# Third feed-forward: rounding the gelu rows on ScalarE, and copying the broadcast gates on VectorE

## The reference, cut to what matters

```python
x = x + _L2_ffn_ref(_layernorm(x, axis=-1), L2_ffn_wg, L2_ffn_w1, L2_ffn_b1, L2_ffn_w2, L2_ffn_b2)

def _L2_ffn_ref(x, wg, w1, b1, w2, b2):     # 8 experts, 128 -> 512 -> 128, top 2
    logits = xt.astype(jnp.float32) @ wg.astype(jnp.float32)
    scores = jax.nn.softmax(logits, axis=-1)
    gvals, gidx = jax.lax.top_k(scores, K)
    ...
    gvals = gvals * keep                    # an expert takes at most cap tokens
```

## Time and profile before

| what | value |
|---|---|
| runs | 4552.9, 4552.88 and 4551.13 us, median 4552.88 us |
| profiled execution | span 4550.5 us; no time outside the span is recorded for it |
| busy over the whole span | PE 90%, DVE 86%, ACT 60%, POOL 32% |
| third feed-forward, main loop | 2002.1 to 2811.0 us of the span, 808.9 us, 16 groups |

### The profile page before, as it was taken

How to read it: one execution, slowest core, us unless ns; L and a number is a source line. 1 busy time by engine, 2 the same in 40 slices (tenths; PEclk the granted TensorE clock), 3 DMA queues, 4 the chain that set the end, 5 groups by cost and what they waited for, 6 DMA issues and landing times. The chain is left out here.

```text
span 4550.5 us, 105158 instructions
## 1 busy us (share of the span) xinstructions
PE 4085.3 (90%) x34134; PEld 2858.5 (63%) x34135; DVE 3902.8 (86%) x7025; ACT 2713.1 (60%) x4836; POOL 1476.4 (32%) x779
## 2 busy tenths in 40 slices
PE   6984789994997999869999997999949999699999
PEld 3562556664774666657777775666636666577777
DVE  7888789997996888779999998888868888688888
ACT  3433577772775777535555554777757777366665
POOL 2210055540004555312111213555525555122222
PEclk9976999995998999869999998999969999699999
DMA  1010022221002222200000000222222221100000
GB/s 59 17 46 1 11 68 63 65 49 49 1 0 57 57 59 58 78 24 1 1 0 1 0 1 23 64 55 60 52 64 47 55 50 47 72 15 14 14 14 14
DMA packets 129636, 162.04 MB, mean 36 GB/s; under 512 B 32972, under 2 KB 88593, under 8 KB 128306
## 3 DMA queue, kind: packets, MB, share of 16 engines
q1 hardware_dynamic: 129457, 159.97, 13.3%
HBM read 36.38 MB, written 8.39 MB: 10 GB/s over the span
## 5 line engine op out<-in xcount | busy, mean ns | idle before, releaser
L709 ACT ACTIVATE a_p<-a_p 128x480 f32<-128x480 f32 x832 | 500.7, 602 | 408.0 <-DVE a_p L551 403.8
L1648 DVE TENSOR_TENSOR f_al<-f_a,f_ah 128x512 fp32r<-128x512 f32 x768 | 690.9, 900 | 17.5
L347 POOL TENSOR_TENSOR a_km<-a_k,a_slots 96x1920 fp32r<-96x1920 f32 x186 | 631.8, 3416 | 180.8 <-DMA a_k<-a_kh 180.8
L546 DVE TENSOR_REDUCE a_mx<-a_sc 128x4 f32<-128x480 f32 (+1 forms) x832 | 543.0, 653 | 140.0 <-PE a_sc L802 108.2
L1728 ACT ACTIVATE f_a<-f_pu,f_b 128x512 f32<-128x512 f32 x512 | 353.4, 690 | 374.1 <-PE f_pu L1231 198.6
L551 DVE TENSOR_TENSOR a_p<-a_sc,a_mx 128x480 f32<-128x480 f32 x832 | 531.8, 639 | 18.8
L715 ACT ACTIVATE a_pt<-a_tp 120x512 f32<-120x512 f32 x832 | 486.4, 585 | 76.3 <-PE a_tp L811 73.8
L811 PE MATMUL a_tp<-ident,a_p 128*120 128x128 f32 x3328 | 511.8, 276 | 12.0 <-ACT a_p L709 9.7
L1611 POOL TENSOR_TENSOR f_ya<-f_ya,f_yg 128x512 f32<-128x512 f32 x192 | 254.0, 1323 | 769.1 <-DVE f_yg L1663 466.6
L811 PEld LDWEIGHTS a_tp<-ident,a_p 128*120 128x120 f32 x3328 | 400.3, 138 | 98.8 <-ACT a_p L709 34.8
L796 PE MATMUL a_sc<-a_km,a_qr 96*128 96x480 f32 x768 | 396.2, 516 | 33.0 <-ACT a_qr L704 31.4
(11 more groups left out here) (403 smaller groups left out, 9394.3 us busy)
## 6 DMA issues: line engine op xcount, KB each, us to landing
a_q<-a_qh SPq DMA_DIRECT2D x384, 64.0 KB, 2.0
a_k<-a_kh SPq DMA_DIRECT2D x384, 60.0 KB, 2.0
a_ctx<-in_ctxT SPq DMA_DIRECT2D x64, 240.0 KB, 2.7
a_q<-a_ql SPq DMA_DIRECT2D x192, 64.0 KB, 2.0
a_k<-a_kl SPq DMA_DIRECT2D x192, 60.0 KB, 2.0
s_k<-s_kh SPq DMA_DIRECT2D x128, 64.0 KB, 2.0
s_q<-s_qh SPq DMA_DIRECT2D x128, 64.0 KB, 2.0
x<-in_x SPq DMA_DIRECT2D x4, 1024.0 KB, 7.9
```

The lines of the kernel that those rows point to most:

```text
L347: v.tensor_tensor(KM[par][:, i, :, :].rearrange("p b (j k) -> p b j k", k=KN), K3[:, i, :, :].unsqueeze(2).to_broadcast([TR, GB, 4, KN]), ...
L546: v.tensor_reduce(mx[:], view, AX.X, ALU.max).then_inc(mx_ready, 1)
L709: a.activation(PR[s % 4][:], PR[s % 4][:], ACT.Exp).then_inc(exp_ready, 1)
L1648: v.tensor_tensor(AL[s % 4][:], A[s % 2][:], AH[s % 4][:].bitcast(F32), ALU.subtract).then_inc(Z["lo_ready"], 1)
```

## The change

In the third feed-forward only, `high` moves from VectorE to ScalarE. There it is called one slot later: after the gelu of slot s ScalarE rounds the rows of unit s - 1, as in the fourth feed-forward. `low` on VectorE follows one slot later too. The copy of the broadcast gates out of PSUM, `spread`, moves from ScalarE to VectorE and stands directly ahead of `weigh` in its program. LAG becomes 3. The tiles and their numbers stay: two `A`, four `AH`, four `AL`, two `PU`. In the diff the first hunk is the shared setting, the next three are VectorE's program, the last is ScalarE's.

```diff
-    LAG = 3 if two else 2
+    LAG = 3
...
-                def high(g, s):
-                    n = g * N + s
-                    dve.wait_ge(Z["a_ready"], n + 1)
-                    at_least(dve, Z["dn_ready"], n - 3)
-                    v.tensor_copy(AH[s % 4][:], A[s % 2][:]).then_inc(Z["hi_ready"], 1)
...
+                def spread(g, u):
+                    if u % HB != 0:
+                        return
+                    e = u // HB
+                    dve.wait_ge(Z["ge_ready"], g * E + e + 1)
+                    at_least(dve, Z["yg_ready"], g * E + e - 1)
+                    v.tensor_copy(GX[e % 2][:], PG[:]).then_inc(Z["gx_ready"], 1)
...
                         if two:
                             product(g, s)
-                            lagged(g, s, first, 1, low)
-                        else:
-                            high(g, s)
-                            low(g, s)
+                        lagged(g, s, first, 1, low)
+                        if not two:
+                            lagged(g, s, first, LAG, spread)
                         lagged(g, s, first, LAG, weigh)
...
                 def group(g, par, first, last):
                     for s in range(N):
                         rows(g, s)
+                        lagged(g, s, first, 1, high)
                         if two:
-                            lagged(g, s, first, 1, high)
-                        lagged(g, s, first, LAG, spread)
+                            lagged(g, s, first, LAG, spread)
```

More of the change, by code:

```diff
@@ L1687, in group @@
                     if last:
-                        if two:
-                            low(g, N - 1)
+                        low(g, N - 1)
                         for u in range(N - LAG, N):
+                            if not two:
+                                spread(g, u)
                             weigh(g, u)
@@ L1759, in group @@
                     if last:
+                        high(g, N - 1)
                         if two:
-                            high(g, N - 1)
-                        for u in range(N - LAG, N):
-                            spread(g, u)
+                            for u in range(N - LAG, N):
+                                spread(g, u)
                 gates_in(0, 0)
```

## The result

The changed kernel takes 4878.2 us (median of 4 runs, 4877.3 to 4880.3) against 4552.6 us before: a ratio of 1.0717, 95% interval 1.0704 to 1.0730. It is 326 us slower. The forecast was 4891 us.

A forecast was written before the change was run, and what follows sets the result against it. VectorE was taken to bound the old kernel, a ring of waits the changed one: 1039 + 74 + 15 + 12 and 7 drain make the loop 1147 us, +338 on 4553, so 4891 us; range 4780 to 4950.

The forecast's parts named there:

- The step that decided: Third feed-forward loop: a circle of waits, not engine rates, sets the pace, 2.03 us a unit against 1.58 before.
- the ring: Third feed-forward: gelu n-1, rounding of n-2, low n-2, then gelu n, with two A tiles; 2.03 us a unit.
- the first rival: Circle of waits doesn't bind; TensorE's rate limits the loop to 775 us, kernel 4519 us; 4 in 100.
- turns of the ring: Loop's 512 units, each gelu, rounding, low and handovers one after another at 2.03 us: 1039 us.
- held by GpSimd, slots other than the split's: VectorE's low stretched 0.66 us when it starts 0.51 us into GpSimd's add; 74 us for all 112.
- slot of the split: Slot 10: weigh, cast and the split's subtraction, which meets an add, end about 0.6 us later than counted.
- slot of the residual: Slot 5: VectorE's residual takes 1.76 us, less 0.08, which is 0.34 us too long for the free time.
- turns of the hardware loop: VectorE's 2.49 us stand behind that slot's copy makes low 1.8 us late, seven times: 12 us.
- drain behind the last gelu: End of the third feed-forward loop: work left after the last gelu, 7 us.
- the line read from the earlier trace: Excess of a held low is about 1.17 us minus its offset into GpSimd's add, from two pairs.
- TensorE's clock: Loop: clock stays 1.00 with TensorE about 80% busy; rival: falls to 1.2 GHz, 5159 us, 6 in 100.
- what LAG does: In the loop, LAG at 3 costs only a slot at the end, under 2 us.

The follow-up runs named there:

- the other order: Changed kernel, two A tiles kept, but ScalarE rounds each unit's rows at once, directly behind that unit's own gelu instead of one slot later: 4517.1 us, ratio 0.9921.

## Why the prediction was right

**The step that decided** held: the loop runs at the ring's turn, not at the highest rate. Four A tiles and the other order each open the ring, by different means, and both give TensorE's bound of the first rival: 4523 and 4517 us, for which it had 4519.

**The terms**, in the changed kernel. The measured ones are read from the gaps between all gelus of the loop: 2.025 us is the undisturbed gap, and what a slot's gaps have above it is added up over the 16 groups.

| term | forecast, us | measured, us |
|---|---|---|
| turns of the ring | 512 x 2.03 = 1039 | 510 x 2.025 = 1032.8, and 0.6 between the first two gelus |
| held by GpSimd, slots other than the split's | 96 x 0.66 = 63 | 58.8, about 0.61 each |
| slot of the split | 16 x 1.26 = 20 | 19.6 |
| slot of the residual | 16 x 0.34 = 5 | 4.5 |
| turns of the hardware loop | 12 | 7.4, with all else that the rows above leave |
| drain behind the last gelu | 7 | 3134.7 - 3125.2 = 9.5 |
| loop | 1147 | 1133.2 |

All terms but the drain came out a little below the forecast, so the 13 us between 4891 and 4878 are a sum of small errors and not of large ones that cancel.

One turn stands in the rows as 0.59 (2502.36 to 2502.95), 0.65 for the rounding and its handover (to 2503.60), 0.69 for `low`, and 0.10 to the gelu at 2504.39: 2.03 us. The hold is as reckoned in 49 of the 96 `low` that met an add: they start 0.50 to 0.52 us into it and take 1.32 to 1.34 us, 0.63 to 0.65 too much, where the forecast had 0.51 and 0.66. One of them:

```profile
2252.36 1.29 POOL L1611 TENSOR_TENSOR f_ya<-f_ya,f_yg 128x512 f32<-128x512 f32 x1 [7.45 <-DVE f_yg L1657]
...
2252.87 1.32 DVE L1642 TENSOR_TENSOR f_al<-f_a,f_ah 128x512 fp32r<-128x512 f32 x1 [0.67 <-ACT f_ah L1737]
```

Another 31, like the one shown in the result, start 0.59 or 0.60 us into the add and are held 0.54 to 0.56 us; by the line read from the earlier trace rows it is 1.17 - 0.60 = 0.57. The rest lie within 0.03 us of the same line. The mean of `low` came out as 801 ns, not 840, because the mean hold is 0.59 us and because only 96 of them are held and not 112: in the split's slot the split is held in its place:

```profile
2517.57 1.32 POOL L1608 TENSOR_TENSOR f_ya<-f_yg 128x512 f32<-128x512 f32 x1 [15.18 <-DVE f_yg L1657]
```

```profile
2517.32 0.42 DVE L1627 CAST f_xh<-f_htall 128x512 fp32r x1
2517.78 1.66 DVE L1629 TENSOR_TENSOR f_xl<-f_htall,f_xh 128x512 fp32r<-128x512 f32 x1
2519.36 0.68 DVE L1642 TENSOR_TENSOR f_al<-f_a,f_ah 128x512 fp32r<-128x512 f32 x1
```

By the Trainium skill's rule (SBUF — State Buffer, "Who interferes with whom") the `low` at 2501.03 would have waited for the add's end at 2501.72, 0.69 us; it was held 0.55. That the two exclude one another agrees, and taking the add out of the way gave 68 us back; the length goes by the rows.

**The term that was mis-sized** is the turn of the hardware loop: 12 us forecast. I had put VectorE's 2.49 us behind the copy of that slot as if they began only when it ended, and seven times, where the trace before has six such stands, 14.8 us in all. (The 1.2 us a group in the forecast's sum for VectorE should therefore be 0.9.) No `low` of the changed kernel shows an idle time put down to issue. How VectorE's turn hides there was not tested. What remains is behind a `low`, ahead of ScalarE's gelu:

```profile
2213.28 0.69 DVE L1642 TENSOR_TENSOR f_al<-f_a,f_ah 128x512 fp32r<-128x512 f32 x1 [1.42 <-ACT f_ah L1737]
2214.34 0.69 ACT L1731 ACTIVATE f_a<-f_pu,f_b 128x512 f32<-128x512 f32 x1 [1.18 <-DVE f_al L1642]
```

The gelu follows the end of `low` by 0.37 us and not by 0.10. The three gaps between gelus at this turn are 2.82, 2.11 and 2.39 us; at the borders of groups without a turn they are 2.60, 2.02 and 2.12. That is 0.6 us a turn, some 4 us in the loop, a part of them in the row of the held slots. What ScalarE does in that time the rows don't say.

**TensorE's clock** held: 1.00 from 2003 to 3125 us, with TensorE 83.5% busy (946.22 of 1133.2 us), where I had said about 80%. Only the first 1.5 us (0.87) and the drain behind the last gelu (0.83 from 3125 to 3130 us, then 0.50) were lower. No swing of the kind that the Trainium skill (TensorE: Matmul & The Clock Gate, "A second HAM failure mode: psum-queue depth-cycling") tells of was seen between them.

**What the forecast left out** is what LAG does once the ring is open. It reckoned LAG as worth under 2 us in the changed kernel. No run has the closed ring with LAG 2, so this is not shown; for it speaks that the chain found with LAG 2 takes 3.23 us for two units, below the 4.05 us of two turns of the ring. With four A tiles LAG 3 is worth 108 us. With the rounding at once it is worth 11 us while the copy is on VectorE, and nothing that can be told with the copy on ScalarE (4517.9 against 4518.4 us). So the change carries one edit that its own order of the rounding would have needed for its aim, if the ring had been open.

## What to carry to other kernels

Before work is moved between engines, write down each ring of waits with its tiles: for every tile that is written again, what must have read it, and what stands ahead of that reader in its engine's program. A step put one slot later on an engine that also starts the ring makes the ring longer by everything between; check the turn against the bound by rate, and if it is longer, either give the first tile more buffers or issue the step at once. Check the smallest edit alone: here the rounding moved without the copy and without LAG, in the right order, gives all of the gain that can be told (0.76%).

## What the runs showed of the hardware that was not expected

The hold between VectorE and GpSimd goes both ways, by who starts first. In the loop of the changed kernel the adds start while VectorE is idle: their mean is 1289 ns, and `low` is the one that is stretched, to a mean of 801. In the loop with four A tiles `low`'s mean is only 706, and the adds pay instead (the group of adds in that kernel):

```profile
L1612 POOL TENSOR_TENSOR f_ya<-f_ya,f_yg 128x512 f32<-128x512 f32 x96 | 165.7, 1726 | 413.2 <-DVE f_yg L1658 413.2
```

In the kernel with four A tiles and LAG 2 an add started 0.10 us into a `low` and took 1.75 us, while that `low` kept its 0.69:

```profile
2432.67 0.69 DVE L1643 TENSOR_TENSOR f_al<-f_a,f_ah 128x512 fp32r<-128x512 f32 x1
2432.77 1.75 POOL L1612 TENSOR_TENSOR f_ya<-f_ya,f_yg 128x512 f32<-128x512 f32 x1 [4.71 <-DVE f_yg L1658]
```
